# Absolute sums of the weights in 134 pieces over four buffers in place of 236 over two

## The chip, the cores and the metric

One Trainium2 chip, all eight cores. Each core runs the same program on its own rows; there is no exchange between them. The metric is device time in microseconds, that of the slowest core.

## The reference

One transformer layer on x of shape (4, 2048, 2048) in float32: grouped-query attention with 16 heads of 128 and 4 key/value groups, causal; a layer norm of x + attention; an FFN with ternary weights; and a layer norm of the sum.

```python
def ternary_quant(w):
    s = jnp.mean(jnp.abs(w))
    q = jnp.clip(jnp.round(w / s), -1.0, 1.0) * s
    return w + jax.lax.stop_gradient(q - w)
...
h1 = jnp.einsum('bsd,hd->bsh', x, w1q)
h3 = jnp.einsum('bsd,hd->bsh', x, w3q)
g = jax.nn.silu(h1) * h3
return jnp.einsum('bsh,dh->bsd', g, w2q)
...
x = _layernorm(x + attn(x, Wq, bq, Wk, bk, Wv, bv), axis=-1)
x = _layernorm(x + ffn(x, w1, w3, w2), axis=-1)
```

w1 and w3 are 5461 x 2048, w2 is 2048 x 5461. The scale of the quantization is the mean of the absolute values over the whole matrix, so every weight has to be read once before the first one can be quantized.

## The kernel before

A core works on one batch element and on 1024 of its 2048 query rows. It stages the work as follows; each engine's program is written out in order, and semaphores (`W` waits, `INC` counts up) tie the engines together.

1. **Projections.** GpSimd's DMA queue loads activations and attention weights with a cast to bf16 (xkvT in two halves, wk, wv, then xqT and one wq per head into two buffers). TensorE makes K, V and Q; VectorE evicts them.
2. **Absolute sums.** At the same time SyncE's queue loads all of w1, w3 and w2 in float32, 129 MB, piece by piece into two buffers of 2752 columns at `F_ABS` in the tensor `af`, and ScalarE takes |.| of each piece in place with `accum_out`, which leaves one partial sum for each partition in a column at `F_PAR`. There are `NABS` = 236 pieces: w1 and w3 in 172 pieces of 128 x 1024, w2 in 64 of 128 x 1376. In DRAM a row of 2048 elements of w1 or w3 is one contiguous run, and a whole 128 x 2048 block is contiguous; a w2 row is 5504 long. Semaphore `ld` counts 16 for each load, `fS` one for each sum.
3. **Attention.** For 16 heads and 16 key chunks: scores (L337), Exp on ScalarE (L388), mask on VectorE (L403), row sums with a matrix of ones and the product with V (L356, L363). In ScalarE's program it stands behind all of the absolute sums. `F_RSB` is a buffer of the row sums, two of 1024 columns.
4. **Scales, residual, layer norm.** VectorE reduces the partial sums to three numbers (`p_fin_vector`), TensorE sums them over the partitions; x is loaded at `F_X1`, the attention is transposed and added, the layer norm (L524 and on) follows, and the result is spilled and transposed.
5. **FFN, first part.** For 43 chunks of hidden columns, w1's and w3's blocks of 128 x 2048 (1 MB) are loaded again (L625) into two buffers each, quantized on VectorE (L644, L647) and multiplied (L684); Silu and product follow. VectorE waits here too, before it quantizes piece ss, for piece ss + 3: `return LD_SPILL + 16 * min(ss + 4, NHC * 2)`.
6. **FFN, second part**, with w2 in 128 pieces of 688 columns (L761, L764, L801), then the second layer norm and the store.

The absolute sums' two waits are these: SyncE, before it issues load i, waits for sum i - 2 (`W(sync, "fS", i - 1)`, L309), and ScalarE, before sum i, waits until load i + 1 has landed (`W(scalar, "ld", LD_CONSTS + 16 * min(i + 2, NABS))`, L317).

Of the kernel before, what the change touches and what calls it, by code (L numbers as in the profile page):

```python
# [11 lines left out]
AX = mybir.AxisListType  # L12
# [42 lines left out]
F_P3 = 296  # L55
# [2 lines left out]
F_RC = 304  # L58
F_X1 = 432
F_ABS = 432  # L60
F_RSB = 5936
F_PAR = 7984
F_W1S = 432
F_W3S = 4528
F_SIL = 8624
# [10 lines left out]
def _build_nc(debug_stage=None):  # L76
# [19 lines left out]
    with contextlib.ExitStack() as ctx:  # L96
# [11 lines left out]
        def INC(instr, name, k=1):  # L108
            instr.then_inc(sems[name], k)
            cnt[name] += k  # L110
            return cnt[name]

        def W(eng, name, val):
            if val > 0:
                eng.wait_ge(sems[name], val)
# [3 lines left out]
        def on(engname, fn):  # L119
            getattr(blk, engname)(fn)  # L120
# [4 lines left out]
        def aff(c0, n):  # L125
            return af[:, c0:c0 + n]
# [15 lines left out]
        LD_CONSTS = cnt["ld"]  # L142
# [152 lines left out]

        abs_pieces = []
        for hc in range(NHC):
            abs_pieces += [("w1", hc, 0, 1024), ("w1", hc, 1024, 1024)]
        for hc in range(NHC):
            abs_pieces += [("w3", hc, 0, 1024), ("w3", hc, 1024, 1024)]  # L300
        for ec in range(NEC):
            abs_pieces += [("w2", ec, q4 * 1376, 1376) for q4 in range(4)]
        NABS = len(abs_pieces)

        def p_abs_sync(sync):
            W(sync, "ld", LD_CONSTS)
            for i, (w, c, o, n) in enumerate(abs_pieces):
                if i >= 2:
                    W(sync, "fS", i - 1)  # L309
                src = {"w1": d_w1, "w3": d_w3, "w2": d_w2}[w]  # L310
                INC(sync.dma_start(out=aff(F_ABS + (i % 2) * 2752, n),
                                   in_=src[c][:, o:o + n]), "ld", 16)
        on("sync", p_abs_sync)

        def p_abs_scalar(scalar):
            for i, (w, c, o, n) in enumerate(abs_pieces):
                W(scalar, "ld", LD_CONSTS + 16 * min(i + 2, NABS))  # L317
                buf = aff(F_ABS + (i % 2) * 2752, n)
                INC(scalar.activation(buf, buf, AF.Abs,  # L319
                                      accum_out=aff(F_PAR + i, 1)), "fS", 1)  # L320
        on("scalar", p_abs_scalar)
        FS_ABS = cnt["fS"]

        def p_att_tensor(tensor):
            W(tensor, "pe", NUNITS)
            W(tensor, "lc", LC_CONSTS)
            for idx in range(257):
# [15 lines left out]
                if idx >= 1:  # L343
# [25 lines left out]
                    if kc == 15:  # L369
                        W(tensor, "rev", h + 1)  # L370
                        last = None
                        for j in range(8):
                            last = tensor.transpose(  # L373
                                psR[:, j * 128:(j + 1) * 128],
                                aff(F_RSB + (h % 2) * 1024 + j * 128, 128), identf)
                        INC(last, "fT", 1)
# [19 lines left out]
        def p_att_vector(vector):  # L396
            W(vector, "lc", LC_CONSTS)
            for idx in range(256):
# [7 lines left out]
                if kc == 15:  # L406
                    W(vector, "av", idx + 1)
                    INC(vector.tensor_copy(aff(F_RSB + (h % 2) * 1024, 1024), psR[:]),
                        "rev", 1)
# [7 lines left out]

        def p_fin_vector(vector):
            W(vector, "fS", FS_ABS)
            vector.reduce_sum(aff(F_P3 + 0, 1), aff(F_PAR + 0, 86), AX.X)  # L420
            vector.reduce_sum(aff(F_P3 + 1, 1), aff(F_PAR + 86, 86), AX.X)
            INC(vector.reduce_sum(aff(F_P3 + 2, 1), aff(F_PAR + 172, 64), AX.X),
                "fV", 1)
        on("vector", p_fin_vector)
        FV_P3 = cnt["fV"]

# [531 lines left out]
```

How the kernel before makes its waits and increments, by code:

```python
        def W(eng, name, val):  # L113
            if val > 0:
                eng.wait_ge(sems[name], val)
# [28 lines left out]
        def ckpt(sync):  # L144
            sync.wait_ge(sems["ld"], cnt["ld"])
            INC(sync.dma_start(out=af[0:1, F_CK:F_CK + 1], in_=d_cf[0:1, 0:1]),
                "lc", 16)
# [47 lines left out]
                def p_gp1(gpsimd):  # L195
                    gpsimd.wait_ge(sems["pm"], 12)
                    for ec in range(NEC):
                        INC(gpsimd.dma_start(
                            out=abf(A_XKV + ec * 1024, 1024),
                            in_=d_xkvT[ec * 128:(ec + 1) * 128, 1024:2048]), "lg", 16)
# [55 lines left out]
        def p_gp2(gpsimd):  # L256
            gpsimd.wait_ge(sems["pm"], 24)
            for ec in range(NEC):
                INC(gpsimd.dma_start(out=abf(A_XKV + ec * 1024, 1024),
                                     in_=d_xqT[ec * 128:(ec + 1) * 128, :]), "lg", 16)
            for h in range(HH):
                if h >= 2:
                    gpsimd.wait_ge(sems["pm"], 24 + (h - 1))
                INC(gpsimd.dma_start(out=abf(A_WQ + (h % 2) * 2048, 2048),
                                     in_=d_wq[h]), "lg", 16)
# [240 lines left out]
            def p_st(sync):  # L506
                W(sync, "fV", wait_v)
                for t in range(8):
                    INC(sync.dma_start(out=d_out[t * 128:(t + 1) * 128, :],
                                       in_=aff(F_X1 + t * 2048, 2048)), "st", 16)
                sync.wait_ge(sems["st"], cnt["st"])
```

## Time and profile before

| | |
|---|---|
| time before, median of 3 runs | 3425.87 us (3425.35 to 3426.92) |
| the profiled execution | 3443.65 us; span of its slowest core 3442.1 us, of the others 3403.9 to 3433.1 us |
| TensorE matmuls busy | 1566.2 us, 46% of the span |
| VectorE busy | 843.1 us, 24% |
| ScalarE busy | 669.7 us, 19% |
| GpSimd busy | 36.8 us, 1% |
| DMA | 331.55 MB, 96 GB/s in the mean |
| chain that ended last | DMA 55%, DVE 18%, ACT 14%, PE 7% |

Read it from the top: the profiled execution is one run, and the trace is of its slowest core, so every duration taken from the trace belongs to 3443.65 us and not to the median. Busy shares are means over all stages. The chain that ended last is the work that set the end, followed back from the last instruction; its shares say what was being waited for, not what was busy.

### The profile page before, as it was taken

The numbers are of one execution on the slowest core, as the hardware profiler recorded it, in microseconds if no ns is written. First come the engines' busy times: TensorE is split into PE (matmuls) and PEld (weight loads), VectorE is DVE, ScalarE is ACT, GpSimd is POOL, SyncE is SP. The second block draws the span as 40 slices with busy tenths as digits, with TensorE's granted clock in tenths as the row PEclk, the third lists the DMA queues.
The fourth block names the chain that finished last, engine by engine and source line by source line (L and its number), as shares of the span: only waits on it lengthen the run. The fifth ranks groups of instructions, "written<-read, shape, count | busy, mean of one in ns | idle before, by whom it ended". The sixth has DMA issues, their size and how long they took to land.

```text
span 3442.1 us, 20622 instructions; the slowest of 8 cores (3403.9 to 3442.1 us)
## 1 busy us (share of the span) xinstructions
PE 1566.2 (46%) x6820; PEld 691.0 (20%) x6820; DVE 843.1 (24%) x1367; ACT 669.7 (19%) x951; POOL 36.8 (1%) x73
## 2 busy tenths in 40 slices
PE   1565560000000003777432788888788255555650
PEld 0222220000000001333212333333333022222220
DVE  0110000000000000222155444444445133333333
ACT  0111222222222224555323000000000000000015
POOL 1010000000000000000000000000000000000000
PEclk9787875555555556999756899999999677777775
DMA  8655443333334442000204333333332422222212
GB/s 151 134 124 128 122 123 108 104 108 105 104 119 129 124 130 66 1 1 1 81 17 142 115 110 112 120 119 114 120 113 86 143 74 73 75 71 74 74 41 98
DMA packets 79885, 331.55 MB, mean 96 GB/s; under 512 B 8870, under 2 KB 9126, under 8 KB 64550
## 3 DMA queue, kind: packets, MB, share of 16 engines
q1 hardware_dynamic: 69846, 305.06, 27.7%
q0 software_dynamic: 9936, 25.17, 4.8%
q8 instruction: 58, 0.95, 0.1%
q14 instruction: 45, 0.37, 0.0%
HBM read 338.58 MB, written 16.78 MB: 103 GB/s over the span
## 4 chain that ended last, share of the span: by engine, by line
DMA 55%; DVE 18%; ACT 14%; PE 7%; issue 5%; SPq 1%; DVEq 0%; ACTq 0%
DMA af<-w_sb 53%; ACT af L319 8%; DVE ab L647 6%; DVE ab L764 3%; DVE ab L644 3%; ACT ab L388 2%; DVE ab L761 2%; PE psR L356 2%; PE psO L363 1%; PE pH L684 1%; DVE ab L403 1%; PE psR L373 1%; DMA af<-xq 1%; DVE af L498 1%; PE psB L337 1%
## 5 line engine op out<-in xcount | busy, mean ns | idle before, releaser
L684 PE MATMUL pH<-ab 128*128 128x512 bf16 x2752 | 641.3, 395 | 158.7 <-DVE ab L656 114.0
L356 PE MATMUL psR<-ab 128*128 128x512 bf16 (+3 forms) x384 | 108.5, 338 | 892.8 <-DVE ab L403 890.7
L319 ACT ACTIVATE af<-af 128x1024 f32<-128x1024 f32 (+1 forms) x236 | 268.0, 1136 | 1021.2 <-DMA af<-w_sb 1021.1
L684 PEld LDWEIGHTS pH<-ab 128*128 128x128 bf16 x2752 | 273.5, 101 | 526.2 <-issue 237.8
L801 PE MATMUL pH<-ab 128*128 128x512 bf16 x1376 | 326.9, 403 | 86.3 <-DVE ab L764 86.3
L403 DVE TENSOR_TENSOR ab<-ab 128x128 bf16<-128x128 bf16 x256 | 57.4, 224 | 1053.6 <-ACT ab L388 1052.6
L356 PEld LDWEIGHTS psR<-ab 128*128 128x128 bf16 x384 | 30.3, 98 | 974.4 <-issue 970.4
L644 DVE TENSOR_SCALAR ab<-af 128x2048 bf16<-128x2048 f32 x86 | 110.6, 1286 | 412.6 <-DMA af<-w_sb 412.6
L647 DVE SCALAR_TENSOR_TENSOR ab<-af,ab 128x2048 bf16<-128x2048 f32 x86 | 202.2, 2352 | 9.4 <-DVE ab L644 0.5
L801 PEld LDWEIGHTS pH<-ab 128*128 128x128 bf16 x1376 | 141.2, 103 | 266.8 <-issue 122.8
L698 ACT ACTIVATE af<-pH,af 128x1024 f32<-128x1024 f32 x43 | 47.9, 1115 | 713.5 <-DVE ab L656 706.1
L761 DVE TENSOR_SCALAR ab<-af 128x688 bf16<-128x688 f32 x128 | 74.0, 578 | 410.5 <-DMA af<-w_sb 410.5
L817 PE MATMUL pH<-af 128*128 128x128 f32 x128 | 27.1, 350 | 236.1 <-DVE af L780 233.0
L829 ACT ACTIVATE af<-pH,af 128x512 f32<-128x512 f32 x32 | 22.0, 687 | 558.6 <-PE pH L817 558.6
L764 DVE SCALAR_TENSOR_TENSOR ab<-af,ab 128x688 bf16<-128x688 f32 x128 | 119.7, 935 | 13.7 <-DVE ab L761 0.5
L388 ACT ACTIVATE ab<-psB,af 128x1024 bf16<-128x1024 f32 (+7 forms) x128 | 94.8, 741 | 93.2 <-PE psB L337 84.2
L363 PE MATMUL psO<-ab 128*128 128x512 bf16 (+3 forms) x384 | 107.4, 336 | 0.0
L388 ACT ACTIVATE ab<-psA,af 128x1024 bf16<-128x1024 f32 (+7 forms) x128 | 94.6, 739 | 43.5 <-PE psA L337 41.3
L214 PE MATMUL psA<-ab 128*128 128x512 bf16 x64 | 17.7, 444 | 114.4 <-DMA ab<-wv_sb 74.7
L817 PEld LDWEIGHTS pH<-af 128*128 128x128 f32 x128 | 19.7, 163 | 243.4 <-issue 239.7
L279 PE MATMUL psA<-ab 128*128 128x512 bf16 x128 | 36.6, 457 | 62.6 <-DMA ab<-wq_sb 62.6
L656 DVE SCALAR_TENSOR_TENSOR ab<-pH,af 128x1024 bf16<-128x1024 f32 x43 | 55.0, 1279 | 14.2 <-PE pH L684 14.2
(90 smaller groups left out, 1075.9 us busy)
## 6 DMA issues: line engine op xcount, KB each, us to landing
af<-w_sb SPq DMA_DIRECT2D x172, 512.0 KB, 3.7
af<-w_sb SPq DMA_DIRECT2D x86, 1024.0 KB, 5.0
af<-w_sb SPq DMA_DIRECT2D x64, 688.0 KB, 4.0
af<-w_sb SPq DMA_DIRECT2D x128, 344.0 KB, 3.0
ab<-xkvT POOLq DMA_DIRECT2D x32, 256.0 KB, 21.0
ab<-wq_sb POOLq DMA_DIRECT2D x16, 512.0 KB, 7.0
af<-xq SPq DMA_DIRECT2D x8, 1024.0 KB, 16.4
x1spill<-af SPq DMA_DIRECT2D x8, 1024.0 KB, 12.6
```

The costliest lines, as they stand in the source:

```text
L319: INC(scalar.activation(buf, buf, AF.Abs, accum_out=aff(F_PAR + i, 1)), "fS", 1)
L356: tensor.matmul(psR[:, b2 * 512:b2 * 512 + n2], ones128, abf(A_PT + OFF[kc] + b2 * 512, n2), start=(kc == 0), stop=stop)
L363: last = tensor.matmul(psO[:, b2 * 512:b2 * 512 + n2], abf(A_VTM + kc * 512 + g * 128, 128), abf(A_PT + OFF[kc] + b2 * 512, n2), start=(kc ...
L388: INC(scalar.activation(abf(A_PT + OFF[kc], N), ps[:, 0:N], AF.Exp, bias=m16col), "ex", 1)
L403: INC(vector.tensor_tensor(pslab, pslab, abf(A_MSK + kc * 128, 128), ALU.mult), "mk", 1)
L644: n1 = INC(vector.tensor_scalar(qq, st, aff(F_UC + uc, 1), None, ALU.is_gt), "bq", 1)
L647: INC(vector.scalar_tensor_tensor(qq, st, aff(F_NUC + uc, 1), qq, ALU.is_lt, ALU.subtract), "bq", 1)
L656: INC(vector.scalar_tensor_tensor(abf(A_G + hc * 1024, 1024), pH[2 + par][:], aff(F_NS + 1, 1), aff(F_SIL, 1024), ALU.mult, ALU.mult), "fg ...
L684: last = tensor.matmul(ps[:, b2 * 512:(b2 + 1) * 512], lhs, abf(A_XKV + ec * 1024 + b2 * 512, 512), start=(ec == 0), stop=(ec == NEC - 1))
L761: n1 = INC(vector.tensor_scalar(qq, st, aff(F_UC + 2, 1), None, ALU.is_gt), "bq", 1)
L764: INC(vector.scalar_tensor_tensor(qq, st, aff(F_NUC + 2, 1), qq, ALU.is_lt, ALU.subtract), "bq", 1)
L801: last = tensor.matmul(ps[:, b2 * 512:(b2 + 1) * 512], lhs, abf(A_G + hc * 1024 + b2 * 512, 512), start=(hc == 0), stop=(hc == NHC - 1))
```

## The change

The pieces are cut larger, and there are four buffers of 2048 columns in place of two of 2752. w1 and w3 go in 86 pieces of 128 x 2048, w2 in 16 times 2048, 2048 and 1408 columns, so `NABS` is 134. SyncE waits, before load i, for sum i - 4; ScalarE waits, before sum i, until load i + 3 has landed. `F_RSB` and `F_PAR` move behind the larger buffers, and the three reductions read as many columns as there are partial sums now.

```diff
-F_RSB = 5936
-F_PAR = 7984
+F_RSB = 10672
+F_PAR = 12720
...
         for hc in range(NHC):
-            abs_pieces += [("w1", hc, 0, 1024), ("w1", hc, 1024, 1024)]
+            abs_pieces.append(("w1", hc, 0, 2048))
         for hc in range(NHC):
-            abs_pieces += [("w3", hc, 0, 1024), ("w3", hc, 1024, 1024)]
+            abs_pieces.append(("w3", hc, 0, 2048))
         for ec in range(NEC):
-            abs_pieces += [("w2", ec, q4 * 1376, 1376) for q4 in range(4)]
+            abs_pieces += [("w2", ec, 0, 2048), ("w2", ec, 2048, 2048),
+                           ("w2", ec, 4096, 1408)]
         NABS = len(abs_pieces)
...
             for i, (w, c, o, n) in enumerate(abs_pieces):
-                if i >= 2:
-                    W(sync, "fS", i - 1)
+                if i >= 4:
+                    W(sync, "fS", i - 3)
                 src = {"w1": d_w1, "w3": d_w3, "w2": d_w2}[w]
-                INC(sync.dma_start(out=aff(F_ABS + (i % 2) * 2752, n),
+                INC(sync.dma_start(out=aff(F_ABS + (i % 4) * 2048, n),
                                    in_=src[c][:, o:o + n]), "ld", 16)
...
             for i, (w, c, o, n) in enumerate(abs_pieces):
-                W(scalar, "ld", LD_CONSTS + 16 * min(i + 2, NABS))
-                buf = aff(F_ABS + (i % 2) * 2752, n)
+                W(scalar, "ld", LD_CONSTS + 16 * min(i + 4, NABS))
+                buf = aff(F_ABS + (i % 4) * 2048, n)
                 INC(scalar.activation(buf, buf, AF.Abs,
                                       accum_out=aff(F_PAR + i, 1)), "fS", 1)
...
             W(vector, "fS", FS_ABS)
-            vector.reduce_sum(aff(F_P3 + 0, 1), aff(F_PAR + 0, 86), AX.X)
-            vector.reduce_sum(aff(F_P3 + 1, 1), aff(F_PAR + 86, 86), AX.X)
-            INC(vector.reduce_sum(aff(F_P3 + 2, 1), aff(F_PAR + 172, 64), AX.X),
+            vector.reduce_sum(aff(F_P3 + 0, 1), aff(F_PAR + 0, 43), AX.X)
+            vector.reduce_sum(aff(F_P3 + 1, 1), aff(F_PAR + 43, 43), AX.X)
+            INC(vector.reduce_sum(aff(F_P3 + 2, 1), aff(F_PAR + 86, 48), AX.X),
                 "fV", 1)
```

## Rows read from the trace of the kernel before

**Rows 1.** The page's slices: busy tenths, granted clock in tenths, GB/s

```profile
PE   1565560000000003777432788888788255555650
PEclk9787875555555556999756899999999677777775
GB/s 151 134 124 128 122 123 108 104 108 105 104 119 129 124 130 66 1 1 1 81 17 142 115 110 112 120 119 114 120 113 86 143 74 73 75 71 74 74 41 98
```

**Rows 2.** Table by stretches: busy us (x instructions), clock, DMA share, GB/s

```profile
0.00:100.00 100.00, 25.30 (x108) 10.99 (x109) 3.85 (x3) 11.62 (x19) 11.42 (x25) 1.00 0.77 146
...
515.00:930.00 415.00, 3.67 (x17) 1.30 (x14) 1.28 (x1) 96.04 (x167) 0.00 (x0) 0.51 0.34 106
...
1345.00:1700.00 355.00, 255.26 (x1275) 115.55 (x1273) 86.20 (x405) 199.00 (x270) 0.00 (x0) 0.92 0.01 2
...
1860.00:2640.00 780.00, 623.04 (x2684) 270.05 (x2683) 362.56 (x300) 44.77 (x40) 0.00 (x0) 0.94 0.35 122
```

**Rows 3.** Chain that ended last, 509 to 515 us: start, us, what

```profile
509.59 3.68 DMA af<-w_sb
...
513.31 0.04 issue
513.35 1.16 ACT af L319 x2
```

**Rows 4.** Timeline of TensorE: start, us, what, [idle before <- releaser]

```profile
519.32 0.59 PE L337 MATMUL psA<-ab 128*128 128x512 bf16 x2 [1.68 <-DVE ab L288]
```

**Rows 5.** Timeline of ScalarE, same columns

```profile
73.21 1.06 ACT L319 ACTIVATE af<-af 128x1024 f32<-128x1024 f32 x1 [17.90 <-DMA af<-w_sb]
...
78.27 1.06 ACT L319 ACTIVATE af<-af 128x1024 f32<-128x1024 f32 x1 [3.91 <-DMA af<-w_sb]
...
135.28 1.06 ACT L319 ACTIVATE af<-af 128x1024 f32<-128x1024 f32 x1 [4.14 <-DMA af<-w_sb]
...
173.23 1.06 ACT L319 ACTIVATE af<-af 128x1024 f32<-128x1024 f32 x1 [4.84 <-DMA af<-w_sb]
...
228.79 1.06 ACT L319 ACTIVATE af<-af 128x1024 f32<-128x1024 f32 x1 [3.85 <-DMA af<-w_sb]
...
271.46 1.06 ACT L319 ACTIVATE af<-af 128x1024 f32<-128x1024 f32 x1 [8.51 <-DMA af<-w_sb]
...
513.35 1.06 ACT L319 ACTIVATE af<-af 128x1024 f32<-128x1024 f32 x1 [3.83 <-DMA af<-w_sb]
...
990.05 1.35 ACT L319 ACTIVATE af<-af 128x1376 f32<-128x1376 f32 x1 [4.02 <-DMA af<-w_sb]
...
1335.94 1.35 ACT L319 ACTIVATE af<-af 128x1376 f32<-128x1376 f32 x1 [4.13 <-DMA af<-w_sb]
...
1338.73 1.28 ACT L388 ACT_TABLE_LOAD   x1
```

**Rows 6.** Waits, 1330 to 1345 us: us in total, times, longest

```profile
PE psR L356 <- DVE ab L403: 821.3, 1, 821.3
```

**Rows 7.** DMA issues: count, KB each, median us to landing

```profile
af<-w_sb SPq DMA_DIRECT2D x172, 512.0 KB, 3.7
af<-w_sb SPq DMA_DIRECT2D x86, 1024.0 KB, 5.0
af<-w_sb SPq DMA_DIRECT2D x64, 688.0 KB, 4.0
```

**Rows 8.** Chain that ended last in the FFN's first part, 73 loads

```profile
1973.56 6.13 DMA af<-w_sb
...
1992.81 4.93 DMA af<-w_sb
2001.72 4.94 DMA af<-w_sb
...
2631.51 4.99 DMA af<-w_sb
```

**Rows 9.** Groups by line: a sum over 2048 columns in the layer norm

```profile
L524 ACT ACTIVATE ab<-af 128x2048 bf16<-128x2048 f32 x16 | 30.6, 1910 | 0.2
```

## The prediction

> **What bounds the kernel now.** I read the page's slices first: from the seventh slice to the fifteenth TensorE does nothing at all, while its granted clock sits at 0.5 [rows 1]. A kernel whose matmul engine rests for a quarter of its time is bound there by something else, so the next view is the table by stretches [rows 2]. It shows from 515 to 930 us PE 3.7 us busy, DVE 1.3 us, and ACT busy for only 96 of 415 us with the DMA at 0.34; the stretch up to 1339 us looks the same in the slices. No engine is full and no bandwidth is used up. Such a stretch is a chain of latencies, and the chain that ended last says which: one load of a weight piece, one ACTIVATE of L319, one load, one ACTIVATE [rows 3].
>
> The whole kernel waits for this chain because ScalarE's program is in order: the first Exp (L388) stands behind the last of the 236 absolute sums. The last sum ends at 1338.7 us and Exp's table is loaded right behind it [rows 5], and PE waited 821 us for it [rows 6]. The projections were through at 519 us: TensorE had made its first two score products (L337) and stopped [rows 4]. Whatever shortens the chain of absolute sums down to that time shortens the kernel one for one; the attention and the two FFN stages behind it are moved as blocks, for nothing in them is touched.
>
> **Why there is a load and a sum in turn, although there are two buffers.** Sum i waits (L317) until load i+1 has landed. Load i+1 may start (L309) when sum i-1 is done. So between sum i-1 and sum i a whole load always lies open: the period is load + sum, not the larger of the two. In [rows 3] that is 3.68 us of load, 1.16 us of ACTIVATE with its accumulator read, and 0.1 us of waits. Over the stretch the starts 513.35 (the sum of index 76) and 990.05 (index 172, the first of w2) give 476.7/96 = 4.97 us a period [rows 5]; w2's go from 990.05 to 1335.94 (62 periods), 5.58 us.
>
> **The change part by part.**
>
> *The waits.* With four buffers, load i+3 waits for sum i-1, and sum i waits for load i+3. Again exactly one whole load lies between two sums. The depth by itself gives no overlap; it only changes the two ends: four loads go out together at the start, and the last four sums run back to back.
>
> *The pieces.* w1 and w3 go from 172 pieces of 512 KB to 86 of 1024 KB, w2 from 64 of 688 KB to 32 of 1024 KB and 16 of 704 KB. So 236 periods become 134. This is where time comes from: the fixed part of a load and of a sum is paid 102 times less.
>
> *Cost of a load of 1024 KB.* The issues show 512 KB landing in 3.7 us, 688 KB in 4.0 and 1024 KB in 5.0 [rows 7]. The 1024 KB ones are those of L625, the very same rows of w1 and w3 with the same kind of turn-taking (there between DVE's quantization and a load), all eight cores at once. Their pieces in the chain are mostly 4.9 to 5.2 us, but some take over 6 [rows 8]. From the first to the last of these rows lie 72 periods, 9.14 us each; a short one is 8.91 us with a load of 4.93 (1992.81 to 2001.72), so the other parts are 3.98 and the mean load is 5.16, say 5.15 us. I take 5.15. The low end is 4.95; for w2's pieces, whose rows are strided, extending the step from 512 to 688 KB (0.3 us for 176 KB) gives even 4.6. For 704 KB I take 4.05, beside 688 KB's: 5.58 - 1.45 - 0.1 = 4.03.
>
> The Trainium skill ("DMA: Bandwidth & Descriptors", Anatomy of one DMA) makes a DMA's time about 2.0 us plus its bytes over 436 GB/s, which is 4.4 us for 1024 KB. The trace's 5.0 is dearer; with the page's figure the estimate would come out 114 x 0.75 = 86 us lower.
>
> *Cost of a sum.* ACTIVATE on 1024 columns takes 1.06 us and on 1376 columns 1.35 us [rows 5], so 0.83 ns a column; 2048 columns give 1.91 us, and a Square of that size in the layer norm takes 1910 ns [rows 9]. With the accumulator read, less the overlap (1.16 for 1.06), that is 2.02 us; for 1408 columns 1.48 us.
>
> *Start.* The first sum now waits for 4 MB. Before, 2.5 MB had landed at 73.2 us [rows 5] through the projections' own loads; the other 1.5 MB come within some 4 us more when nothing stops the queue (1.3 us for each further 512 KB, [rows 7]). First sum at 79 us.
>
> *Clean sum.* Loads 4 to 133: 82 x (5.15 + 0.1) = 430.5, 32 x 5.25 = 168, 16 x 4.15 = 66. Sums: 118 x 2.02 = 238 and 16 x 1.48 = 24. Together 927 us, so the end would be at 1006 us.
>
> *Contention with the projections.* From 78.27 (index 4) to 990.05 (index 172) the old chain took 911.8 us where 168 clean periods of 4.97 are 835: 77 us are lost while GpSimd's queue loads activations and weights. One sees where: from 135.28 to 173.23 only four steps, from 228.79 to 271.46 four, and from 271.46 to 513.35 42 steps at 5.76 us, while in between they take 5.0 [rows 5]. GpSimd's queue moves the same bytes as before, so its bursts last about as long; the loss in them grows a little because a large piece meets them. Scaling the two bursts by bytes gives 24 + 28 us, and 36 for the stretch of the sixteen wq loads (18, 23 and 33 before); together I take 88. Ends: 60 if fewer loads mean fewer collisions, 156 if each piece pays double.
>
> *The end of the chain* is then 79 + 927 + 88 = 1094 us against 1338.7: 245 us less. This lies well behind the projections' end at 519 us, so these stay covered even if the heavier stream delays them; the cover would be gone only after 570 us of delay.
>
> *The rest.* F_RSB and F_PAR move to free columns; the three reductions read 43, 43 and 48 columns in place of 86, 86 and 64, nanoseconds either way. The last loads into the four buffers (up to column 8624) are done before Exp starts, and x's rows are loaded over them only after the attention. SP's queue has nothing behind these loads until the attention's end. Nothing.
>
> **Sum.** The profiled execution took 3443.65 us around a span of 3442.1; with 245 less it is 3199. It lies 17.8 us over the median of the runs, 3425.87. A saving in a chain of fixed steps carries over: 3425.87 - 245 = 3181 us.
>
> **The rivals.**
>
> *A. As worked out*, 3181 us. Its own bounds: loads of 4.95 (4.66 for w2's) and 60 us of contention take off 32 + 28, so 3121; all the contention doubled adds 68, so 3249.
>
> *B. A load's time goes with its bytes* (the other side). If eight cores that stream 1 MB pieces get in each other's way at the memory, 1024 KB could take twice 3.7 = 7.4 us. That is 114 x 2.25 = 257 us more than in A: the end of the chain at 1351 us, 12 us after the old one, 3438 us in all. w2 gives the loss, as four pieces of 5.58 become two of 9.5 and one of 5.6. It decides from 5.15 + 245/114 = 7.3 us a load. For it: in the bursts a 512 KB load takes over 9 us, so loads do stretch. Against it: in the FFN the same 1 MB loads land in 5.0 with all cores at 122 GB/s; the new chain would ask about 1 MB in 7.27 us, 144 GB/s, and slice 0 moved 151 [rows 1]. Chance 3 in 100.
>
> *C. Real overlap.* If the four buffers did let loads run ahead, the chain would go at the pace of streaming, some 2.6 us a megabyte (twice 1.3, [rows 7]), or of the sums at 2.02. 129 MB would be through by about 79 + 335 + 88 = 502 us, the projections' end at 519 would bound, and the kernel would take about 3426 - 820 = 2606. Against it stand the waits as read above: sum i asks for load i+3, which asks for sum i-1. Chance 1 in 100. The Trainium skill ("Trainium Kernel Development and Optimization", Best Practices) says to double-buffer so that DMA and compute overlap; the trace, with two buffers and 3.8 us of idle ACT before each sum, doesn't show that buffers alone do it.
>
> *D. The projections' stretch gives nothing.* If up to 515 us bytes move only as fast as before (39.5 MB by then), the gain is only in the clean part: 46.5 x 7.27 + 32 x 7.27 + 16 x 5.63 + 8 = 669 us after 515, an end at 1184 and 3271 us. For it: these loads share the DMA engines with GpSimd's, at a share of 0.77 in the first 100 us. Against: half of that time the steps take the clean 5.0 us. Chance 7 in 100.
>
> *E. The clock.* The granted clock rose to 0.92 in the attention after a rest at 0.5 [rows 2]. With a shorter rest I see no reason for another; were it to stay at 0.5 in the FFN's 780 us, where PE is busy 623 at 0.94, this would cost over 300 us and make the kernel slower. Chance 1 in 100.
>
> **Chances.** A 88, D 7, B 3, C and E 1 each. Range 3125 to 3235: A's bounds but for their outer ends, cut where D begins. A measurement of this kernel tells 0.2%, some 7 us, from no change; B could land there or just above it: faster 0.96, same 0.01, slower 0.03.
>
> **What the profile after should show.** L319 134 times, with a largest ACTIVATE of 1.91 us; ACT's idle before one about 5.3 us in the clean stretch, for a period near 7.3; the chain still load and sum in turn; first Exp near 1095 us; PE's wait before it about 570 us; attention, layer norm and FFN stretches as long as before. If the mean load is off 5.15 by 0.1, the time is off by 11 us; it is wrong altogether if the load of 1024 KB isn't what the FFN's is.

## The result, and the profile after

The kernel after takes 3135.66 us (median of 8 runs, 3127.61 to 3150.67), the kernel before 3428.14 (8 runs beside it). The ratio is 0.914, its 95% interval 0.9125 to 0.9163: 292 us less, where 245 were forecast; 3135.66 lies in the stated range, 11 us above its lower end. Runs in which the cores of one die took over 1% longer than the others at a lower granted clock are left out of every time here. The profiled execution took 3127.86 us, with a span of 3126.3 on its slowest core, and the line numbers from the sums on are one higher than before.

The page's slices (busy tenths of TensorE, granted clock in tenths, GB/s) answer to [rows 1]:

```profile
PE   0763554000000577754268888888882555555560
PEclk9976777555555899985689999999996777777775
GB/s 193 148 169 181 164 163 164 148 147 138 143 143 144 23 1 1 1 69 40 95 147 114 115 121 110 120 121 109 120 95 139 77 72 73 73 73 76 72 32 107
```

TensorE's empty stretch is six slices long in place of nine, and the memory moves 138 to 148 GB/s in them where it moved 104 to 130. The table by stretches answers to [rows 2] (us; busy us of PE, PEld, DVE, ACT, POOL, each with its instructions; clock, DMA share, GB/s):

```profile
555.00:930.00 375.00, 0.00 (x0) 0.00 (x0) 0.00 (x0) 106.19 (x111) 0.00 (x0) 0.50 0.42 144
1037.00:1390.00 353.00, 254.50 (x1281) 113.99 (x1279) 86.07 (x406) 199.75 (x270) 0.00 (x0) 0.93 0.00 1
...
1555.00:2330.00 775.00, 624.61 (x2670) 269.30 (x2670) 359.01 (x275) 45.84 (x41) 0.00 (x0) 0.93 0.35 122
```

The attention and the FFN are what they were: the same work at the same clock, moved to the left. The clock came back to 0.93 after the shorter rest as it had to 0.92. The chain that ended last shows load and sum still in turn (start, us, what), beside [rows 3]:

```profile
606.61 4.92 DMA af<-w_sb
611.53 0.02 issue
611.55 0.02 ACTq L115
611.57 0.04 issue
611.62 2.01 ACT af L320 x2
```

The load takes 4.9 us where 5.15 was taken, and ScalarE's idle time before a sum is about 5.0 us where 5.3 was forecast. And the timeline of ScalarE, beside [rows 5] (start, us, what, [idle before <- releaser]):

```profile
43.87 1.91 ACT L320 ACTIVATE af<-af 128x2048 f32<-128x2048 f32 x1
...
80.50 1.91 ACT L320 ACTIVATE af<-af 128x2048 f32<-128x2048 f32 x1 [18.36 <-DMA af<-w_sb]
...
137.33 1.91 ACT L320 ACTIVATE af<-af 128x2048 f32<-128x2048 f32 x1 [5.01 <-DMA af<-w_sb]
...
184.09 1.91 ACT L320 ACTIVATE af<-af 128x2048 f32<-128x2048 f32 x1 [7.53 <-DMA af<-w_sb]
...
240.83 1.91 ACT L320 ACTIVATE af<-af 128x2048 f32<-128x2048 f32 x1 [5.01 <-DMA af<-w_sb]
...
288.96 1.91 ACT L320 ACTIVATE af<-af 128x2048 f32<-128x2048 f32 x1 [7.06 <-DMA af<-w_sb]
...
738.71 1.91 ACT L320 ACTIVATE af<-af 128x2048 f32<-128x2048 f32 x1 [5.16 <-DMA af<-w_sb]
...
1026.72 1.38 ACT L320 ACTIVATE af<-af 128x1408 f32<-128x1408 f32 x1 [4.07 <-DMA af<-w_sb]
...
1033.35 1.28 ACT L389 ACT_TABLE_LOAD   x1
```

These are the sums of index 0, 2, 10, 14, 22, 26, 86 (w2's first) and 130; the last three run back to back behind it. The chain's end has moved from 1338.7 to 1033.3 us, 305 us; the part behind it is 2093 us long on this core and was 2103 on the other kernel's slowest. The two profiled executions differ by 316 us, the medians by 292: that of before was 15.5 us above its median over 8 runs, that of after 7.8 us below. On the eight cores the last accumulator read begins at 1317 to 1339 us before and at 1023 to 1033 after.

TensorE's last projection and its first score product, beside [rows 4] (start, us, what):

```profile
519.57 7.07 PE L279 MATMUL psO<-ab 128*128 128x512 bf16 x32
528.29 0.59 PE L338 MATMUL psA<-ab 128*128 128x512 bf16 x2 [1.65 <-DVE ab L288]
```

The projections end at 527 us and not at 518. TensorE's wait before the first row sum is 507 us long. The forecast had said about 570 us; the difference is the 61 us by which the chain ended earlier than forecast and these 9.

### The profile page after: what moved, and what is told of

The parts are those of the page before. It is cut to its first block, busy times and chain, and to the rows that moved or that the text cites. A ratio compares the mean times of both kernels' runs of the same rounds, so it can differ in the third digit from the quotient of the medians.

```text
span 3126.3 us, 20110 instructions; the slowest of 8 cores (3103.5 to 3126.3 us)
## 1 busy us (share of the span) xinstructions
PE 1571.6 (50%) x6820; PEld 690.6 (22%) x6820; DVE 842.6 (27%) x1367; ACT 639.4 (20%) x747; POOL 36.8 (1%) x73
## 4 chain that ended last, share of the span: by engine, by line
DMA 52%; DVE 20%; ACT 14%; PE 8%; issue 5%; SPq 1%; DVEq 1%; ACTq 0%
DMA af<-w_sb 50%; ACT af L320 8%; DVE ab L648 6%; DVE ab L765 4%; DVE ab L645 3%; ACT ab L389 3%; DVE ab L762 2%; PE psR L357 2%; PE psO L364 1%; DVE ab L404 1%; PE pH L685 1%; PE pH L601 1%; DVE af L499 1%; DMA af<-xq 1%; PE psR L374 1%
## 5 line engine op out<-in xcount | busy, mean ns | idle before, releaser
L685 PE MATMUL pH<-ab 128*128 128x512 bf16 x2752 | 644.0, 396 | 151.3 <-DVE ab L657 110.2
L320 ACT ACTIVATE af<-af 128x2048 f32<-128x2048 f32 x134 | 247.3, 1845 | 730.0 <-DMA af<-w_sb 730.0
L818 PE MATMUL pH<-af 128*128 128x128 f32 x128 | 26.8, 347 | 233.2 <-DVE af L781 230.1
L601 PE MATMUL pH<-af 128*128 128x128 f32 x128 | 25.1, 314 | 70.0 <-DVE af L565 70.0
## 6 DMA issues: line engine op xcount, KB each, us to landing
x1spill<-af SPq DMA_DIRECT2D x8, 1024.0 KB, 12.2
```

The source lines that it names most:

```text
L320: INC(scalar.activation(buf, buf, AF.Abs, accum_out=aff(F_PAR + i, 1)), "fS", 1)
L601: INC(tensor.transpose(slot, aff(F_X1 + t * 2048 + ec * 128, 128), identf), "fT", 1)
L685: last = tensor.matmul(ps[:, b2 * 512:(b2 + 1) * 512], lhs, abf(A_XKV + ec * 1024 + b2 * 512, 512), start=(ec == 0), stop=(ec == NEC - 1))
```

## The experiments

All ratios are to the kernel before in runs on the same chip. The experiments ran on three chips. The kernel before took 3438.39 us on that of experiments 1, 2, 3 and 5, 3441.53 on that of 6, 7 and the first kernel of 8, and 3429.77 on that of 4, the second kernel of 8, and 9. So a difference in us between kernels of two chips is uncertain by some 10 us; their ratios are the better measure.

**1. The depth alone.** Four buffers with the waits of after, and the pieces of before:

```diff
-            abs_pieces.append(("w1", hc, 0, 2048))
+            abs_pieces += [("w1", hc, 0, 1024), ("w1", hc, 1024, 1024)]
...
-            abs_pieces += [("w2", ec, 0, 2048), ("w2", ec, 2048, 2048),
-                           ("w2", ec, 4096, 1408)]
+            abs_pieces += [("w2", ec, q4 * 1376, 1376) for q4 in range(4)]
```

> The 236 pieces of before in four buffers with the waits of after. Theory (one whole load always lies between two sums, and the gain is that of fewer, larger periods): the clean period stays at 4.97 us and w2's at 5.58; only the ends change, 8 us at the end (two more sums without a load before them) and up to some 20 us at the start, where four loads are queued at once: 3395 to 3420 us, 3405 as one number. Rival (the four buffers bring the gain, through overlap or a better share of the DMA engines): the period falls towards 3.7 us or less and the time towards 3140 us.

3438.75 us, ratio 0.9997 (0.9982 to 1.0012). There is no gain at all. The expectation of 3405 us, 21 us less than before, missed; the interval allows 6. In the one trace of each, the table for Exp is loaded at 1307 to 1329 us on the eight cores, where the kernel before has 1317 to 1340, so the 8 us expected at the end may be there; the times do not show them, and why stays open. Its chain, 700 us from the start:

```profile
700.01 3.69 DMA af<-w_sb
...
703.78 1.16 ACT af L319 x2
...
705.00 3.63 DMA af<-w_sb
```

The same load, the same sum, the same order as in [rows 3]. Four buffers overlap nothing here.

**2. The pieces alone.** The 134 pieces in two buffers, with the waits of before:

```diff
-                if i >= 4:
-                    W(sync, "fS", i - 3)
+                if i >= 2:
+                    W(sync, "fS", i - 1)
...
-                W(scalar, "ld", LD_CONSTS + 16 * min(i + 4, NABS))
-                buf = aff(F_ABS + (i % 4) * 2048, n)
+                W(scalar, "ld", LD_CONSTS + 16 * min(i + 2, NABS))
+                buf = aff(F_ABS + (i % 2) * 2048, n)
```

> The 134 pieces of after in two buffers of 2048 columns with the waits of before. Theory: the clean period is that of after, 7.1 us, and what is lost is two loads at the end (9 us) and some 10 us at the start: 3150 us, between 3140 and 3170. Rival (the depth brings a good part of it): over 3250 us.

3139.37 us, ratio 0.9145 (0.911 to 0.918), as the kernel after, and just below the range given: the 19 us expected for the ends do not show. The whole gain is that of the piece's size. ScalarE's idle time before the sums, in the groups by line (busy, mean ns | idle before), is 743.1 us where the kernel after has 730.0 and the one before 1021:

```profile
L320 ACT ACTIVATE af<-af 128x2048 f32<-128x2048 f32 x134 | 247.3, 1846 | 743.1 <-DMA af<-w_sb 743.1
```

**3. Smaller pieces.** As after, but 512 columns a piece, 520 pieces:

```diff
-            abs_pieces.append(("w1", hc, 0, 2048))
+            abs_pieces += [("w1", hc, q * 512, 512) for q in range(4)]
...
+            abs_pieces += [("w2", ec, q * 512, 512) for q in range(10)]
+            abs_pieces.append(("w2", ec, 5120, 384))
```

> Four buffers and the waits of after, but 520 pieces, of 512 columns (256 KB) and in w2 one in eleven of 384. Theory (a load has a fixed part that each period pays): 344 KB land in 3.0 us and 512 KB in 3.7, so 256 KB in about 2.7; with a sum of 0.73 and 0.1 of waits the period is 3.5 us, the chain ends near 1960 us, and the kernel takes about 4050 us, between 3900 and 4150. Rival (a load's time goes with its bytes, 1.85 us for 256 KB): a period of 2.7 us and about 3600 us.

4187.02 us (one run), 37 us above the range given. The fixed part is there. In w1 and w3 it is larger than extrapolated: the load takes 2.9 us and not 2.7, and the period is 3.9 us. In w2 the period is the expected 3.5, with pieces of the same 256 KB; why they land sooner there was not tested. From the chain:

```profile
898.20 2.91 DMA af<-w_sb
...
901.19 0.73 ACT af L320 x2
```

**4. Larger pieces.** Two buffers and the waits of before, but 4096 columns, two blocks of w1 or w3 in one load (the lines added to the kernel before, in part):

```diff
+            if hc % 2 == 0:
+                abs_pieces.append(("w1", hc, 0, 4096 if hc + 1 < NHC else 2048))
...
+            abs_pieces += [("w2", ec, 0, 4096), ("w2", ec, 4096, 1408)]
...
+                        in_=src[c:c + 2].rearrange("b p f -> p b f")), "ld", 16)
```

> The same waits as in before (two buffers, load i+1 lies between the sums), but pieces of 4096 columns (2 MB, two blocks of w1 or w3 in one load), 76 pieces in all: w1 and w3 in 21 pairs and one single each, w2 in 4096 and 1408. Theory (a load is a fixed part plus 1.3 us for each 512 KB): a load of 2 MB takes 4.95 + 2.6 = 7.55 us, its sum 3.73, the period is 11.4 us, 5.7 a megabyte in place of 7.1; the clean chain is 155 us shorter than that of after: about 2985 us, between 2950 and 3030. Rival (past 1 MB a load's time goes with its bytes, so 9.9 us): a period of 13.7 us, and a gain of under 40 us on after.

2995.43 us, ratio 0.874 (0.8713 to 0.8763): 140 us less than after, with load and sum still in turn. The chain:

```profile
571.24 7.27 DMA af<-w_sb
...
578.59 3.72 ACT af L327 x2
...
582.38 7.38 DMA af<-w_sb
```

So four sizes of w1's and w3's loads stand in clean stretches: 256 KB 2.91 us, 512 KB 3.65, 1024 KB 4.92, 2048 KB about 7.35. From 1 to 2 MB that is 2.43 us a megabyte, some 430 GB/s, and what is left at no bytes is 2.5 us. (It is a straight line through two sizes; the 256 KB load lies 0.2 us below it.) The Trainium skill ("DMA: Bandwidth & Descriptors", Anatomy of one DMA) gives 2.0 us plus bytes over 436 GB/s, as a fit for DMAs that GpSimd issues; the loads here are SyncE's. The slope agrees with the trace. The fixed part is half a microsecond short of it at 512 KB and above.

**5. One semaphore for each buffer.** The pieces and buffers of after, but sum i waits for load i alone:

```diff
-                                   in_=src[c][:, o:o + n]), "ld", 16)
+                                   in_=src[c][:, o:o + n]), "la%d" % (i % 4), 16)
...
-                W(scalar, "ld", LD_CONSTS + 16 * min(i + 4, NABS))
+                W(scalar, "la%d" % (i % 4), 16 * (i // 4 + 1))
```

> The pieces and the four buffers of after, but each buffer has a semaphore of its own, so that sum i waits for load i alone and the three loads after it run ahead. Theory (the wait for load i+3, not the number of buffers, kept loads and sums in turn): the chain goes at the pace of streaming, 2.6 us a megabyte, or of the sums, 2.02; with the projections' 48 MB beside it the sums end at 520 to 620 us, the attention starts there in place of 1035, and the kernel takes 2630 to 2760 us, 2680 as one number. Rival (the loads themselves can't go faster under eight cores, at 144 GB/s each they are near what the memory gives): above 3050 us.

2785.99 us, ratio 0.8098 (0.8085 to 0.811): 350 us less than after, but 106 above the one number and 26 above the range. The DMA slices and GB/s, then the timeline of ScalarE and of TensorE:

```profile
DMA  9999999821000003053333333333242222222203
GB/s 226 270 306 287 329 273 315 255 37 23 1 1 1 1 12 110 0 212 107 120 108 119 121 120 113 114 121 107 78 156 72 71 76 72 71 71 75 72 15 121
```

```profile
120.69 1.91 ACT L321 ACTIVATE af<-af 128x2048 f32<-128x2048 f32 x1 [0.45 <-DMA af<-w_sb]
...
123.18 1.91 ACT L321 ACTIVATE af<-af 128x2048 f32<-128x2048 f32 x1 [0.48 <-DMA af<-w_sb]
...
545.40 1.38 ACT L321 ACTIVATE af<-af 128x1408 f32<-128x1408 f32 x1 [2.08 <-DMA af<-w_sb]
...
686.22 1.28 ACT L390 ACT_TABLE_LOAD   x1 [139.35 <-PE psA L339]
...
676.82 7.07 PE L280 MATMUL psO<-ab 128*128 128x512 bf16 x32
```

From 118 to 128 us, between two bursts of GpSimd's loads, a megabyte goes through every 2.5 us with 0.5 us of idle time; over the whole chain it is 3.9 us in the mean. The sums end at 547 us, as expected. What the expectation had wrong is who comes last then: the DMA engines are full (tenths of 9 through seven slices), GpSimd's loads of wq wait among them, and the projections end at 684 us where they had ended at 527. The prediction had put 570 us of cover beside the projections; here nothing is left of it, for they end 157 us later than in after and 137 us behind the sums. ScalarE waited 139 us for the first score product. TensorE's waits for wq, while the sums still run and after them:

```profile
525.43 9.11 PE L280 MATMUL psB<-ab 128*128 128x512 bf16 x32 [11.10 <-DMA ab<-wq_sb]
...
560.22 8.78 PE L280 MATMUL psO<-ab 128*128 128x512 bf16 x32 [5.63 <-DMA ab<-wq_sb]
```

**6. The same with the small pieces of before** (the diffs of 5 and 1 together).

> Four buffers with a semaphore each, and the 236 pieces of before (512 and 688 KB). Theory: once loads run ahead, what a period pays is the sum alone (1.22 us for 512 KB with its wait, 2.4 us a megabyte) or the stream (2.6 us a megabyte), so the size of a piece hardly matters: within 60 us of the same kernel with the large pieces, 2640 to 2800 us. Rival (large pieces are better as such): over 200 us slower than the large pieces with a semaphore each.

2747.14 us (median of 3), ratio 0.7973 (0.7937 to 0.801): 39 us less than with the large pieces, 43 by the ratios. The size that brought all of the gain brings nothing once loads run ahead. Beside experiment 1 this kernel differs in the semaphores alone: with the pieces of before they are worth 0.9997 against 0.7973, some 690 us. The sums end at 624 us and the projections at 638, in better balance:

```profile
622.90 1.35 ACT L320 ACTIVATE af<-af 128x1376 f32<-128x1376 f32 x1 [1.88 <-DMA af<-w_sb]
...
640.09 1.28 ACT L389 ACT_TABLE_LOAD   x1 [15.74 <-PE psA L338]
```

**7. The sums after the projections.** As after, with the loads held back until the last projection's matmuls:

```diff
             W(sync, "ld", LD_CONSTS)
+            W(sync, "pm", NUNITS)
```

> The kernel after, with the loads of the absolute sums held back until the last projection's matmuls are done. It measures what the chain and the projections cost each other. Theory (63 us of the chain of after are lost to GpSimd's loads, and the projections lose little): the projections end at 450 to 520 us, the chain lasts 134 clean periods, some 910 us, without a step over 8 us, and the kernel takes about 3500 us. Rival (the large pieces themselves sometimes take 9 us and more, whatever else is loaded): steps of 8.8 us stay in the chain, which lasts 970 us or more.

3500.84 us (one run). The timelines of TensorE and ScalarE:

```profile
468.37 7.07 PE L279 MATMUL psO<-ab 128*128 128x512 bf16 x32
...
492.42 1.91 ACT L321 ACTIVATE af<-af 128x2048 f32<-128x2048 f32 x1
...
1399.44 1.28 ACT L390 ACT_TABLE_LOAD   x1
```

The projections end at 475 us alone, at 518 beside the sums of before and at 527 beside those of after. From the first sum to the table load lie 907 us, and no step is over 7.7; in the kernel after it is 989. The 82 us between are the price of the projections' loads (one run of this kernel, and one trace of each).

**8. The FFN's waits too.** The semaphores of 5, and the same edit for the four buffers of w1 and w3 and the two of w2:

```diff
-                    W(vector, "ld", ld_fa(hc, w))
+                    W(vector, "wa%d" % (2 * (hc % 2) + (w == "w3")),
+                      16 * (hc // 2 + 1))
...
-                    W(vector, "ld", ld_fb(i))
+                    W(vector, "wb%d" % (i % 2), 16 * (i // 2 + 1))
```

> The kernel with a semaphore for each of the four buffers of the absolute sums, and in the FFN one for each of the four buffers of w1 and w3 and of the two of w2, so that VectorE quantizes a piece when that piece has landed. Theory (the same wait holds these stages too): in the first part a pair of pieces takes the 15 us of its 64 matmuls in place of 18.2, 43 times, in the second an ec the 23 us of its matmuls in place of 38, 16 times: some 130 and 220 us less than the version with the absolute sums' semaphores alone, about 2330 us, between 2250 and 2450. Rival (the FFN is held by VectorE or by TensorE's clock, not by the wait): less than 100 us off.

2306.57 and 2313.54 us, near the 2330 expected. But the expectation's terms, 130 and 220 us off experiment 5's 2786, make 2436, so its number and its terms do not go together, and both terms were too small. From its first matmul to its last the FFN's first part shrank from 773 us in experiment 5 to 596, and the second part from 602 to 332. The first part's group of matmuls (busy, mean ns | idle before), which in the kernel after sat idle for 151.3 us:

```profile
L689 PE MATMUL pH<-ab 128*128 128x512 bf16 x2752 | 596.8, 380 | 10.3 <-DVE ab L652 10.3
```

Then with the small pieces in the sums:

> A semaphore for each buffer in the absolute sums and in both parts of the FFN, with the 512 and 688 KB pieces of before in the sums. In the version with 1 MB pieces the projections ended at 684 us and bound the attention's start, with the small pieces at 632. Theory (the two changes touch different stretches and add): 37 to 50 us less than with 1 MB pieces and all semaphores, whose undisturbed runs took 2307 and 2314 us: 2265 us, between 2240 and 2290. Rival (the difference of the small pieces is lost in the FFN version): 2300 us or more.

2266.12 us, ratio 0.6608 (0.6594 to 0.6623), as expected. The table by stretches, in the FFN's first part:

```profile
1300.00:1800.00 500.00, 476.01 (x2172) 216.65 (x2215) 282.76 (x169) 38.97 (x35) 0.00 (x0) 0.98 0.39 146
```

TensorE is busy 476 of 500 us at a clock of 0.98, where it was 623 of 780 in [rows 2]; a few matmuls are missing from this trace (2696 of 2752 are in it), so the share is higher still. That stage is bound by matmuls now.

**9. And wq's two buffers.** The kernel before this with a semaphore for each buffer of wq:

```diff
-                    W(tensor, "lg", LG_XQ + 16 * min(h + 2, HH))
+                    W(tensor, "lg", LG_XQ)
+                    W(tensor, "lq%d" % (h % 2), 16 * (h // 2 + 1))
```

> As the version before, and the two buffers of wq have a semaphore each, so that projection h waits for wq h and not for wq h+1. Theory (the projections' wq loop has load and matmul in turn by the same kind of wait, but the DMA engines are full in this stretch and the absolute sums end at 623 us): the projections end up to 60 us earlier, the sums don't, and the gain is 0 to 30 us. Rival (the projections alone set the attention's start): 50 us or more.

2249.47 us (median of 4), ratio 0.6562 (0.6539 to 0.6585): the best version, 886 us below the kernel after, and 17 us below the version before it. TensorE's timeline:

```profile
615.53 1.01 PE L359 MATMUL psR<-ab 128*128 128x512 bf16 x2 [129.54 <-DVE ab L406]
```

The projections end at 483 us and not at 633: 150 us earlier where at most 60 were expected. TensorE now waits 130 us for the sums, whose end has not moved (611 us without and 613 with this edit). So the attention begins its row sums at 615.5 us and not at 638.1, and the gain stays small: the sums bind here.

## Why the prediction was right

**The bound and the wait.** Right, and shown from three sides: undoing the pieces leaves 0.9997, undoing the depth leaves 0.9145, and taking the wait for load i+3 away brings the overlap that neither did. Rival C, that the four buffers let loads run ahead, fell with experiment 1. Its price of 2606 us, for the case that they do, was 180 us too low by experiment 5, since it held the projections' end at 519 us, and they ended at 684.

**The load goes with its bytes (rival B).** Refuted by 4.92 us at 1 MB and 7.35 at 2 MB. The mechanism of the gain, 102 fixed parts fewer, is confirmed by experiments 3 and 4 on both sides of the change.

**The projections' stretch gives nothing (rival D).** Refuted: at the sum of index 26, 288.96 us, 30 MB had landed, where the kernel before had some 19.

**The clock (rival E).** 0.93 in attention and FFN.

**The size of the gain.** The end of the chain was put at 1094 us and came at 1033, 61 us earlier. The mechanism was right, and each term of the sum was a little too dear, all on the same side:

- *The load of 1024 KB*, taken as 5.15 us from the FFN's mean, is 4.92 in the chain; with sum and waits the period is 7.09 us and not 7.27 (the mean over w1 and w3 in experiment 7, with no other load about; the clean stretch of after gives 7.08). Over the 84 periods from index 2 to 86 this is 15 us. The 6 us loads of [rows 8] don't appear in the sums' clean stretch; what makes them in the FFN stays open.
- *w2*: 44 periods from 738.71 to 1026.72 are 288.0 us, 6.55 each, where 7.27, 7.27 and 5.63 make 6.72: 8 us.
- *The start.* The sum of index 2 began at 80.5 us, so 6 MB had landed; I had index 0 at 79 us. Two periods of 7.27 us were gained and 1.5 us lost, which makes 13 us. The first burst of GpSimd's loads costs time by the step and hardly by the byte: the first sum waited for 4 MB and began at 43.9 us, where before only 2.5 MB had landed at 73.2.
- *Contention.* Taken as 88 us, it was 658.2 - 84 x 7.09 = 63 us behind index 2. The step that failed is the scaling of bursts by bytes (24 and 28 us, which come out if a burst lets the same bytes pass as before). From 137.33 to 184.09 us four steps of 1 MB took 46.8 us, 18 over their clean time; the second burst, 240.83 to 288.96, 20 over. Before it was 18 and 23 with 512 KB, in experiment 3 23 and 22 with 256 KB, in experiment 4 18 and 20 with 2 MB. A burst costs the chain some 20 us whatever the size, while from 1 MB (256 KB loads) to 6 MB (2 MB loads) pass in it. The stretch of the wq loads cost the other 24 us and not 36, a term that stood without a working.

13 + 15 + 25 + 8 make the 61. That the medians show 47 us more than forecast and not 61 is the spread of the runs: before's profiled execution lay above its median and after's below, by 23 us together, and the part behind the chain was 10 us shorter on the core shown. I can't say which of the two is chance. A forecast of 3181 us less these 61 would be 3120, just below the stated range; that the median lies inside it is in part luck.

**What lies beside.** The reductions, the moved buffers and SP's queue cost nothing that the trace shows; the projections lost 9 us to the heavier stream (518 to 527), which is hidden.

## What to carry to other kernels

Before you add buffers to a load loop, write down which load the consumer waits for and what that load waits for: if a whole load always lies between two uses, depth changes nothing, and only the number of periods or the wait itself does. Here one semaphore counted all loads, and the consumer waited for the count of every load issued so far. One semaphore for each buffer frees it: that was worth 350 us on top of the 292 of the larger pieces, and some 690 us with the old pieces, where these were no longer needed. No run waits on the shared semaphore for the count of load i alone, so whether that would do is not shown. Once loads run ahead, look for who shares the DMA engines: the next bound was the projections' loads, 157 us late, and smaller pieces, which had been the trouble, were then the better ones by some 40 us.

## What the runs showed of the hardware that I had not expected

- A burst of sixteen of GpSimd's loads costs a chain of single loads about 20 us (18 to 23), at 256 KB as at 2 MB a load. The second burst has the first wq loads right behind it.
- With loads running ahead on all eight cores, a core moved 303 GB/s in the mean between 300 and 545 us, and up to 329 in a slice, where the chained loads had moved 144; a 1 MB load of SyncE issued in that stretch took 12.2 us (median) from issue to landing, where it took 4.9 alone.
- Under that stream GpSimd's loads took longer too: a wq load held TensorE up for 10.5 to 12.0 us, and for 5.6 to 6.0 us once the sums had ended. Beside the chained loads of after it had been 6.4 to 7.0 us.
